# Output projections' evictions, and one query's, ahead of the step's maximum on VectorE, in the first two attentions of a four-layer gated block

## The reference, cut to what matters

```python
q = (latents @ Wq).reshape(b, q_len, N_KV_HEADS, N_GROUPS, HEAD_DIM)   # 32 heads of 128
k = (hidden_states @ Wk).reshape(b, kv_len, N_KV_HEADS, HEAD_DIM)      # 4 key heads, context + latents
v = (hidden_states @ Wv).reshape(b, kv_len, N_KV_HEADS, HEAD_DIM)
scores = jnp.einsum('bqhgd,bkhd->bhgqk', q, k) * scale
attn = jax.nn.softmax(scores.astype(jnp.float32), axis=-1).astype(q.dtype)
out = jnp.einsum('bhgqk,bkhd->bqhgd', attn, v)
return out.reshape(b, q_len, N_HEADS * HEAD_DIM) @ Wo
```

## Time and profile before

| | |
|---|---|
| median of 3 executions | 1303.97 us |
| lowest, highest | 1296.91, 1304.06 us |
| the profiled execution | 1296.22 us |
| its span | 1294.5 us |
| TensorE, VectorE, ScalarE, GpSimd busy | 92%, 70%, 49%, 40% of the span |
| steps of the first attention | 29.5 to some 554 us of the span |
| steps of the second attention | 625 to some 909 us |

### The profile page before, as it was taken

One profiled execution on the slowest core, in us unless ns is written; L12 is line 12 of the kernel. 1 busy time (PEld: TensorE's weight loads), 2 busy tenths in 40 slices (PEclk: granted clock), 3 DMA queues, 4 the chain that ended last, 5 costly groups with the idle time before them and its releaser, 6 DMA issues.

```text
span 1294.5 us, 19370 instructions
## 1 busy us (share of the span) xinstructions
PE 1197.0 (92%) x7154; PEld 936.9 (72%) x7154; DVE 909.0 (70%) x1682; ACT 637.1 (49%) x1046; POOL 516.1 (40%) x385
## 2 busy tenths in 40 slices
PE   6999999989999989989989889997899999999986
PEld 5878788868888777777868779786775444777733
DVE  6688789866798899864577856885456774543287
ACT  3556556634566455631454534564235778323252
POOL 5136364725245457444151714232635000355212
PEclk9999999999999989999999989998998999999999
DMA  5578779945689577840376936877212000482000
GB/s 187 114 153 168 145 158 171 201 90 114 135 156 187 115 151 144 161 118 21 91 164 115 200 76 116 149 133 149 61 69 75 1 1 2 129 195 74 1 1 33
DMA packets 356188, 146.38 MB, mean 113 GB/s; under 512 B 327744, under 2 KB 334048, under 8 KB 356096
## 3 DMA queue, kind: packets, MB, share of 16 engines
q1 hardware_dynamic: 356096, 145.15, 53.6%
HBM read 57.17 MB, written 5.37 MB: 48 GB/s over the span
## 4 chain that ended last, share of the span: by engine, by line
PE 37%; DVE 7%; ACT 2%; issue 2%; POOL 1%; DMA 1%; SPq 0%; DVEq 0%; ACTq 0%; POOLq 0%
PE ps L863 5%; PE ps L1993 5%; PE ps L1559 3%; PE ps L1585 3%; PE ps L891 3%; PE ps L832 3%; PE ps L2006 2%; DVE p L1146 2%; DVE rows_and_turned L1133 2%; PE ps L2291 1%; PE ps L1541 1%; PE ps L817 1%; PE ps L808 1%; PE ps L1570 1%; PE ps L1493 1%
## 5 line engine op out<-in xcount | busy, mean ns | idle before, releaser
L863 PE MATMUL ps<-kT,qT 128*128 128x512 f32 (+3 forms) x1152 | 240.6, 344 | 40.8 <-DVE p L1146 38.3
L863 PEld LDWEIGHTS ps<-kT,qT 128*128 128x128 f32 (+1 forms) x1152 | 201.0, 191 | 97.0 <-DVE p L1146 43.5
L987 ACT ACTIVATE ps<-ps,rows_and_turned 128x768 f32<-128x768 f32 x192 | 168.0, 875 | 193.7 <-DVE rows_and_turned L1133 193.7
L995 ACT ACTIVATE p<-ps,rows_and_turned 128x768 f16<-128x768 f32 x192 | 172.9, 900 | 166.8 <-ACT ps L987 101.3
L1133 DVE TENSOR_REDUCE rows_and_turned<-ps 128x1 f32<-128x768 f32 x192 | 183.3, 955 | 96.4 <-PE ps L863 96.4
L891 PE MATMUL ps<-pT,vv 128*128 128x256 f16 (+1 forms) x1728 | 225.7, 277 | 10.4 <-DMA pT<-p 7.0
L1146 DVE SCALAR_TENSOR_TENSOR p<-ps,rows_and_turned,p 128x768 f16<-128x768 f32 x192 | 193.5, 1008 | 7.0 <-ACT p L995 7.0
L891 PEld LDWEIGHTS ps<-pT,vv 128*128 128x128 f16 (+1 forms) x1728 | 169.8, 108 | 31.7 <-issue 14.0
L726 POOL TENSOR_TENSOR wo<-raw,one 128x512 fp32r<-128x512 f32 (+1 forms) x48 | 50.2, 1047 | 252.7 <-PE ps L832 222.0
L817 PE MATMUL ps<-xT,wq 128*128 128x512 f32 x528 | 144.0, 408 | 0.0
L832 PE MATMUL ps<-wo,oT 128*128 128x512 f32 (+1 forms) x396 | 114.9, 416 | 3.1 <-DVE x L1035 3.1
(11 more groups left out here) (276 smaller groups left out, 1933.8 us busy)
## 6 DMA issues: line engine op xcount, KB each, us to landing
raw<-in_l_wq SPq DMA_DIRECT2D x44, 256.0 KB, 3.4
f2raw<-in_f_w SPq DMA_DIRECT2D x11, 776.0 KB, 4.7
rows_and_turned<-in_m_w SPq DMA_DIRECT2D x11, 768.0 KB, 5.5
raw<-in_l_wo SPq DMA_DIRECT2D x32, 256.0 KB, 3.3
pT<-p SPq DMA_TRANSPOSE x192, 3.7
raw<-in_l_wo SPq DMA_DIRECT2D x16, 192.0 KB, 3.3
w3gu<-rows_and_turned SPq DMA_DIRECT2D x11, 256.0 KB, 2.8
ctxraw<-in_ctxT SPq DMA_DIRECT2D x2, 1024.0 KB, 7.7
```

The source lines that it names most:

```text
L863: last = nc.tensor.matmul(sc[:, lo:hi], query(A, h, qp)[:, r * P:(r + 1) * P], keys(A, h // A.g)[0:hd, kp, b, lo:hi], start=(qp, kp) == PA ...
L987: nc.scalar.activation(score_banks(n), score_banks(n), ACT.Exp, bias=nmax[:, n % 32:n % 32 + 1], accum_out=rsum[:, n % 32:n % 32 + 1]).the ...
L995: nc.scalar.activation(p16[:, n % 3, HI], score_banks(n), ACT.Copy, scale=rden[:, n % 32:n % 32 + 1]).then_inc(sem("att_half"), 1)
```

## The change

The list `soon` grows in two ways: every output projection of the step before is in it, and, in a scale step, a query whose bank is 4. So VectorE evicts these ahead of the step's maximum, and no longer behind the remainder. Nothing changes on the other engines.

```diff
-            taken = [self.bank[j] for j in inner_jobs]
-            self.soon[n] = [j for j in before_it if j[0] == "V" or (j[0] == "Q" and self.bank[j] in taken)]
+            taken = [self.bank[j] for j in inner_jobs] + ([4] if n in self.scale_steps else [])
+            self.soon[n] = [j for j in before_it if j[0] in "OV" or (j[0] == "Q" and self.bank[j] in taken)]
```

## The result

The changed kernel takes 1285.39 us, median of 4 executions (1284.36 to 1288.05); the kernel before took 1303.22 us (4 executions, 1296.91 to 1304.06, three of them those of the table above the prediction). The ratio is 0.9875, with a 95% interval of 0.9845 to 0.9905: 1.25% faster, some 16 us, and just beyond the 1% within which I had put the likeliest case (0.63). The profiled execution took 1288.05 us (span 1286.3), against 1296.22 (span 1294.5): there the gain is 8.2 us, half of the timed one.

A forecast was written before the change was run, and what follows sets the result against it. TensorE, busy 92% of the span, was taken as the bound, with gains only where it waits for VectorE. Terms 6.7 + 2.5 - 1.2 + 1.4 + 1.2 + 1.2 = 11.8 us off the 1303.97 median gave 1292, range 1283 to 1302.

The forecast's parts named there:

- Ordinary steps: Steps where the moved eviction fits while TensorE computes the same step's scores: 0 us; a run's first maximum some 0.05 late.
- The query: Scale step of each attention: the transpose waits less for the query's eviction, by 1.80 and 1.79 us.
- The projection behind it: Output projection after the scale step: its wait for the eviction of the one before goes, 3.1 us in both attentions.
- the scale chain: VectorE's value-scale work before the first key projection: 5.06 us against TensorE's 5.28, so it barely does not bind.
- Overload: Steps 101 and 109, where TensorE waits for the remainder: the early eviction delays it 0.60 us each, 1.2 us lost.
- Key steps: Five places where scores wait about 0.28 us for a key's eviction: those waits go, 1.4 us gained.
- Ends: Last step of each attention: the chain from denominator to weighted sum starts 0.60 us earlier, 1.2 us in all.
- GpSimd against VectorE: Four steps where L1073 would start ahead of a blocking GpSimd operation: 2.4 us if so, half taken, 1.2.
- The clock: TensorE's granted clock behind the scale-step waits would rise: 2.5 us gained, bounds 0 and 5.1.
- Rival (d): GpSimd blocks small VectorE instructions elsewhere; three or four new blocks of 1 to 3 us cancel the gain: about 1303, chance 0.10.

The follow-up runs named there:

- few_moves: Changed kernel, but only two queries and 21 output projections evicted early, 67 left late: 1282.8 us, 1.45% faster than the kernel before.
- no_overload: Changed kernel, but in steps 101 and 109 the output projection is evicted where it was before the change: 1285.5 us.
- after_near: Changed kernel, with the two halves of the block maxima of step 100 (and 108) spread over two steps, 100 and 101 (108 and 109): 1283.7 us.
- before_fill: Kernel before, order untouched, with 16 unread products put ahead of the transpose in the scale step: 0.31% faster than the kernel before.
- after_fill: Changed kernel, with 9 unread products put ahead of the transpose in the scale step: 1281.9 us, 1.39% faster than the kernel before.
- key_steps: Changed kernel, but only output projections in steps with a key projection among their inner jobs are evicted early: 0.23% faster than the kernel before.
- o_only: Changed kernel, but only the output projections are evicted early, the scale step's query late: 0.86% faster than the kernel before.

## Why the prediction came out right, step by step

The direction, the waits and the range held. The measured 1.25% is 16 us of 1303, with an interval of 12 to 20 us, above my sum (11.8) and about at my upper end (15.6); against the mean of the 62 later executions of before it is 14.4 us. I was right about which waits go. That the total came so near owes something to errors that cancel, and a few us of it stay open. By its steps:

- **Ordinary steps, 0:** right. few_moves leaves 67 of them out and loses nothing that can be timed. The two traces begin 0.22 us apart (the first maximum at 29.51 and 29.73), which has to be taken off such comparisons: the maximum of step 13 is then not late, those of steps 15 and 16 are late by 0.25 and 0.23, where I had 0.05.
- **The query, 3.6 us:** the two waits fell by 1.53 and 1.64 us, 3.2 in all (5.0 for 8.2). In the first attention the missing part is VectorE's own: its small instructions ahead of the step (L1062 to L1066) took 0.27 us longer, which the eviction does not change.
- **The projection behind it, 3.1 us:** right; the wait is gone, and the scale chain does not bind (0.13 us of margin).
- **Overload, 1.2 us lost:** right in the waits, 0.62 and 0.61 us. That the whole 1.2 us is lost in time is not shown, as no_overload says.
- **Key steps, 1.4 us:** right in kind, mis-sized by half. The five steps are 0.51 to 0.54 us shorter, 2.6 us. I had summed the idle times (0.28), and these hang on modelled ends. Start to start shows it: in the kernel before, from the last projection (285.82) to the scores (287.73) it is 1.91 us, in the changed kernel between the same lines 1.46 (282.47 to 283.93).
- **Ends, 1.2 us:** right. In the first attention TensorE resumes 8.38 us behind the last maximum (549.01 to 557.39), before 8.95 (551.31 to 560.26); in the second 8.42 (899.94 to 908.36), before 8.97: 1.1 us in all.
- **GpSimd against VectorE, 1.2 us:** wrong, it gave nothing. Measured from the GpSimd operation that it meets, L1073 came 0.14 us earlier (0.04 us behind its start, before 0.18), not 0.35, since the maximum ahead of it came 0.23 us late and a small gap stands in front of the denominator. It missed the free place by 0.04 us.

```profile
99.19 2.07 DVE L1073 SCALAR_TENSOR_TENSOR rows_and_turned<-rows_and_turned 128x768 f32<-128x768 f32 x1
```

```profile
99.15 1.30 POOL L729 TENSOR_TENSOR wo<-raw,wo 128x512 fp32r<-128x512 f32 x1
```

  VectorE's instruction took 2.07 us, where the median is 0.95. The rule of the Trainium skill ("SBUF — State Buffer", "SBUF: two separate sides", an exclusive lock that whoever starts first holds) agrees with that row: GpSimd's operation had started first. It was my start time that failed, so no run here tests the 2.4 us that the rule would have given.
- **The clock, 2.5 us:** about right at the place that I meant, and too small for the whole execution. At the place: from the maximum of step 59 to that of step 64, and in the second attention from step 27 to step 32, the changed kernel's trace is 3.69 and 5.16 us shorter than that of before. Of these 8.85 us the two key steps in them take 1.05 and the waits 6.3, which leaves 1.5 us for the clock; in few_moves, no_overload and after_near, with the same moves there, it leaves 1.5 to 2.9. All of these are set against one trace of before. And it does not come every time: the table of before_fill has the lower level behind the changed kernel's wait in 7 of 12 cases, and its own trace has it in both attentions.

  For the whole execution: over the 62 executions of the kernel before, time and mean granted clock go together with a correlation of -0.86 and 0.77 us for each 0.001 of clock. The changed kernel's mean clock is 0.9838 for 0.9776, by that line 4.8 us. The two steps cannot be all of it: 5.1 us was the most that they lost, which is 0.0039 of the span, and the clock rose by 0.0062, over four executions, with 0.002 between the sets of before. Put to the same clock (1285.8 + 2.9 us at 0.980, against 1298.4), the changed kernel is 9.7 us faster, and my sum without the clock term was 9.3. That is luck in part: the terms as measured (3.2, 3.1, 1.2 lost, 2.6, 1.1 and 0) add up to 8.8.

  A stretch that the change does not touch shows how the clock makes two traces differ. It lies some 53 us behind the second attention. Its granted clock, its first group of products and the first of L1595, in the kernel before and then in the changed one:

```profile
967.00:984.00 17.00, 16.50 (x62) 9.84 (x60) 9.44 (x15) 7.08 (x13) 9.14 (x8) 0.60 0.75 229
...
967.22 0.50 PE L1559 MATMUL ps<-k3T,q3T 64*128 64x512 f32 x2
...
1009.47 0.66 PE L1595 MATMUL ps<-ident,oT 128*128 128x128 f32 x4
```

```profile
961.00:978.00 17.00, 16.36 (x82) 9.93 (x81) 13.36 (x21) 9.07 (x17) 9.14 (x8) 1.00 0.79 235
...
961.41 0.51 PE L1559 MATMUL ps<-k3T,q3T 64*128 64x512 f32 x2
...
998.75 0.66 PE L1595 MATMUL ps<-ident,oT 128*128 128x128 f32 x4
```

  The same work takes 42.25 us at a clock of 0.60 in its first 17 us, and 37.34 at 1.00. There is nothing between: it takes 42.1 to 42.3 us in five of the 14 traces (before, before_fill, no_overload, after_near, after_fill) and 37.3 to 37.4 in the other nine, and both values occur on the same chip. So the 8.2 us of the traces are not half of the timed gain. They are 5.6 us by the end of the second attention (913.94 to 908.36, L891), 0.2 us up to this stretch, 4.9 us in it, and 2.5 us given back behind it. And of what the two scale steps gave, 2.7 us are lost again between steps 32 and 46 of the second attention; few_moves, which moves nothing between its steps 33 and 62, loses 2.8 there too, so they are not the price of the moves. One pair of traces tells which waits went, but not the size of the gain. That the profiled execution of before is one of its faster ones (13 of the 62 are faster), and that of the changed kernel the slowest of its four, agrees.

  The measured terms and the clock behind the scale steps make 10 to 12 us, the timed gain is 14 to 16. The rest, within the noise of four executions or in the clock elsewhere, stays open.
- **Rival (d), new blocks:** not shown. The instructions of L1062, L1064, L1066 and L1073 are stretched by 19.3 us in all in the trace of before and by 22.3 in that of the changed kernel, summed over what each takes beyond its shortest. But before has the least of all 14 traces (19.3 to 23.0), and before_fill and key_steps, with few or no moves, have 21.0 and 20.7, so it cannot be put down to the change.

The o_only surplus stays open in part: 5.6 us of waits and 3.2 us for its clock (0.9817 for 0.9776, at 0.77 us per 0.001) make 8.8 of the 11.2 us; the interval reaches down to 7.8.

## What to carry to other kernels

An eviction that another engine waits for belongs ahead of a long reduction whose input is not there yet: it is free where the engine would idle, and where the engine is behind it makes the next wait longer by its full length. A few moves picked by the list of waits do all that ninety do, as far as it can be timed. Idle times that hang on modelled ends are to be measured from start to start, and two traces are to be set to the same start first. Before a pair of traces is read for the size of a gain, the mean granted clock of both executions belongs beside that of all the timed ones, and the stretches that the change does not touch are to be compared first: here one of them held 4.9 of 8.2 us.

## What the runs showed of the hardware

With an unchanged program, the mean granted TensorE clock of an execution lies anywhere between 0.966 and 0.986, and the time between 1293.1 and 1308.5 us with it (62 executions on four chips). One stretch takes either some 42.2 or some 37.4 us, in code that is the same in all kernels here. Behind a wait of TensorE of 4.0 to 4.3 us its next products ran slow in 5 of 6 cases, behind 2.0 to 2.6 us in 7 of 12, and behind at most 1.2 us, or a filled wait, in none of 10. Sixteen products that nobody reads, put into each of two idle stretches of 4 us, make a kernel 0.3% faster (0.06 to 0.56). And a VectorE instruction on 48 numbers per partition, 0.17 us by itself, takes up to 2.75 us beside a long GpSimd operation; the longest of its 11 executions is 2.75 us in every one of the 14 traces.
